# Output projection as seven half products per pair of blocks, with features on partitions

## The reference

```python
qkv = silu(x @ qkv_w.T)                    # 32 heads x (q, k, v) x 128
attn = linear_attention(q, k, v, decay)    # causal, no softmax
xf = attn * rsqrt(mean(attn * attn) + EPS) # over all 4096 features
gate = sigmoid(x @ gate_w.T)
x = layernorm(x + (gate * (norm_w * xf)) @ out_w.T)   # 4096 -> 512
x = layernorm(x + ffn(x))                  # 512 x 512 base, 8 low rank experts, router
```

## Time and profile before

| | us |
|---|---|
| median of three runs | 1011.59 |
| the profiled execution | 1010.33 |
| its span, first to last instruction | 1008.5 |
| TensorE busy | 994.7 |
| VectorE busy | 765.4 |
| ScalarE busy | 662.9 |
| GpSimd busy | 344.3 |

### The profile page before, as it was taken

How to read it: one execution, slowest core, us unless ns; L and a number is a source line. 1 busy time by engine, 2 the same in 40 slices (tenths; PEclk the granted TensorE clock), 3 DMA queues, 4 the chain that set the end, 5 groups by cost and what they waited for, 6 DMA issues and landing times.

```text
span 1008.5 us, 15712 instructions
## 1 busy us (share of the span) xinstructions
PE 994.7 (99%) x5620; PEld 873.8 (87%) x5620; DVE 765.4 (76%) x1102; ACT 662.9 (66%) x1108; POOL 344.3 (34%) x329
## 2 busy tenths in 40 slices
PE   8999999999999999999999999999999999999996
PEld 6878998889888898889988898888988899888886
DVE  6777875787857966778757878578677787699885
ACT  6577754787467764677647874677647786477644
POOL 1453232441443223432323414342224323321462
PEclk9999999999999999999999999999999999999999
DMA  6111121111211111111111102111111121110402
GB/s 209 34 59 57 51 70 43 50 50 30 71 43 50 50 56 49 60 50 58 53 54 58 50 30 71 42 50 51 50 50 63 40 68 51 42 51 22 147 22 84
DMA packets 48813, 57.77 MB, mean 57 GB/s; under 512 B 4320, under 2 KB 40032, under 8 KB 48736
## 3 DMA queue, kind: packets, MB, share of 16 engines
q1 hardware_dynamic: 48736, 56.77, 18.1%
HBM read 54.65 MB, written 2.10 MB: 56 GB/s over the span
## 4 chain that ended last, share of the span: by engine, by line
PE 92%; DVE 2%; ACT 2%; issue 1%; POOL 1%; DMA 1%; SPq 0%; POOLq 0%; ACTq 0%; DVEq 0%
PE ps L1834 20%; PE ps L1835 19%; PE ps L1836 19%; PE ps L1828 10%; PE ps L1829 9%; PE ps L1830 9%; PE ps L1926 2%; PE ps L1941 1%; PE ps L1928 1%; PE ps L1943 1%; DMA acc<-xt 1%; DMA stage<-stream 0%; DVE xl L1030 0%; POOL rstd L1726 0%; ACT wh L388 0%
## 5 line engine op out<-in xcount | busy, mean ns | idle before, releaser
L1834 PE MATMUL ps<-xh,wh 128*128 128x512 f32 x658 | 261.9, 398 | 0.6 <-ACT stg L436 0.6
L1835 PE MATMUL ps<-xl,wh 128*128 128x512 f32 x658 | 257.2, 391 | 0.0
L1836 PE MATMUL ps<-xh,wl 128*128 128x512 f32 x658 | 256.1, 389 | 0.0
L1743 POOL TENSOR_TENSOR stage<-stage 128x512 f32<-128x512 f32 x61 | 85.6, 1403 | 323.6 <-DMA stage<-stream 323.3
L1763 POOL TENSOR_TENSOR sqacc<-sqacc,sq 128x512 f32<-128x512 f32 x64 | 92.4, 1444 | 279.0 <-ACT sq L547 279.0
L1030 DVE TENSOR_TENSOR wl<-stage,wh 128x1024 fp32r<-128x1024 f32 (+2 forms) x145 | 155.7, 1084 | 32.6 <-ACT wh L388 32.5
L388 ACT ACTIVATE wh<-stage 128x1024 fp32r<-128x1024 f32 (+2 forms) x145 | 122.1, 855 | 55.8 <-PE ps L1830 33.7
L1836 PEld LDWEIGHTS ps<-xh,wl 128*128 128x128 f32 x658 | 123.6, 188 | 26.6
L1834 PEld LDWEIGHTS ps<-xh,wh 128*128 128x128 f32 x658 | 123.6, 188 | 24.1 <-issue 1.0
L1835 PEld LDWEIGHTS ps<-xl,wh 128*128 128x128 f32 x658 | 123.9, 188 | 22.0
L1834 PE MATMUL ps<-wh,xh 128*128 128x256 f32 (+1 forms) x416 | 121.0, 291 | 0.0
(11 more groups left out here) (201 smaller groups left out, 2193.7 us busy)
## 6 DMA issues: line engine op xcount, KB each, us to landing
stage<-stream SPq DMA_DIRECT2D x61, 384.0 KB, 3.3
stage<-stream SPq DMA_DIRECT2D x42, 256.0 KB, 2.9
stage<-stream SPq DMA_DIRECT2D x63, 128.0 KB, 2.1
dec<-decay SPq DMA_DIRECT2D x32, 192.0 KB, 2.3
acc<-xt SPq DMA_DIRECT2D x8, 256.0 KB, 6.2
v<-x SPq DMA_DIRECT2D x8, 256.0 KB, 5.6
out<-acc SPq DMA_DIRECT2D x8, 256.0 KB, 2.0
sfull<-lora_router SPq DMA_DIRECT2D x1, 512.0 KB, 4.7
```

The costliest lines, as they stand in the source:

```text
L1743: nc.gpsimd.tensor_tensor(stage[:, s, 1:5:3, :], stage[:, s, 0:6:5, :], stage[:, s, 7:8, :].broadcast_to([P, 2, U]), ALU.add).then_inc(t_p ...
L1834: nc.tensor.matmul(dst, wt[0], mv_[0], start=start, stop=False, skip_group_check=True)
L1835: nc.tensor.matmul(dst, wt[0], mv_[1], start=False, stop=False, skip_group_check=True)
L1836: return nc.tensor.matmul(dst, wt[1], mv_[0], start=False, stop=stop, skip_group_check=True)
```

## The change

The projection of the groups 0 to 6 becomes one product by the same seven-product scheme, transposed: out_w's blocks are stationary, y's token halves move (512 columns), and the result has features on partitions. It is done for two halves j of the 512 output features; the half products (i, j) go to banks 0 to 3 (j = 0) and 4 to 7 (j = 1).

- oa and ob are loaded as blocks with unit sums. ScalarE multiplies them in `stage` by the norm weight before GpSimd's sums (`scale_rows`, eight copies of 256 columns a group).
- The seven operands of y are made of sums by GpSimd (`y_sums`, four operations of 1024 columns) and split 1024 columns at a time (`operand_hi`, `operand_lo`), into yh/yl and, once the scores are done, kh/kl and qh/ql.
- ScalarE copies banks onward (`o_u2_copy`, `o_u3_copy`). Product 5 isn't saved: VectorE adds it out of its bank to two quarters of the sum at once (`out_add` with p5), the others from theirs.
- The ring of weight slots gets a new layout (period of 70 units a group). va and vb, oa and ob are split as A, A, B, B. va's half B moves from QK3 to the next QK0; oa's and ob's halves B are split in the output stage, and `splits_of_load` lets SP reload their places only then; gate weights go there.
- The sum is turned in the tail: `turned(t)`, four transposes for each of 8 token tiles, read by `scaled`. x's tiles `res` take the place of acc there; `last_addition` goes.
- In `scores` the two matmuls of the second key tile come before the last of the first.

Below, "..." stands for what is left out.

```diff
+OUT_STEPS = [(1, 0), (1, 1), (5, 0), (6, 0), (6, 1), (5, 1), (2, 0), (2, 1), (7, 0), (7, 1), (3, 0), (3, 1), (4, 0), (4, 1)]
...
             def v1(g):        # ScalarE
                 n, h = block_no(g, V1), HG * g
                 u2_copy(n)
                 v21_out(n - 1)
+                part(h - 1, 1)
+                square(h - 1, 1)
                 p5_copy(n)
-                if g > 0:
-                    out_rows_hi(g, "oa", 0)
+                sums_hi(g, "oa", "A")
                 u3_copy(n)
-                if g > 0:
-                    out_rows_hi(g, "oa", 1)
                 v11_out(n)
+                sums_hi(g, "ob", "A")
                 v22_out(n)
...
                 scores_hi(h, 0)
+                operand_hi(g, 5)
                 v12_out(n)
                 v21_out(n)
-                values_hi(h)
+                operand_hi(g, 6)
 
             def output(g):    # ScalarE
                 h = HG * g
+                o_u2_copy(g, 0)
+                scores_hi(h, 1)
+                o_u2_copy(g, 1)
+                operand_hi(g, 2)
+                sums_hi(g, "oa", "B")
+                sums_hi(g, "ob", "B")
+                o_u3_copy(g, 0)
+                operand_hi(g, 7)
+                o_u3_copy(g, 1)
+                operand_hi(g, 3)
+                operand_hi(g, 4)
+                values_hi(h)
                 sums_hi(g, "g01", "A")
...
+            def out_add(g, name, j):
...
+                if name == "p5":
+                    dst = acc_t[:, 2 * j + 1, :].rearrange("p (e n) -> p e n", e=2)
+                    nc.vector.tensor_tensor(dst, dst, ps[:, bank, :].unsqueeze(1).broadcast_to([P, 2, W]), ALU.add)\
+                        .then_inc(o_added, 1)
+                    return
...
             def v1(g):        # VectorE
...
+                sums_lo(g, "oa", "A")
                 mask(h, 0)
+                mask_sum(h, 0)
                 c22_add(n)
-                mask_sum(h, 0)
+                sums_lo(g, "ob", "A")
                 c12_add(n)
...
                 scores_lo(h, 0)
+                operand_lo(g, 5)
                 mask(h, 1)
+                mask_sum(h, 1)
+                operand_lo(g, 6)
 
             def output(g):    # VectorE
                 h = HG * g
+                scores_lo(h, 1)
+                operand_lo(g, 2)
+                out_add(g, "p5", 0)
+                sums_lo(g, "oa", "B")
+                sums_lo(g, "ob", "B")
+                operand_lo(g, 7)
+                out_add(g, "c11", 0)
+                out_add(g, "p5", 1)
...
+            def y_sums(g):    # GpSimd
+
+                h = HG * g
+                a11, a12, a21, a22 = y_full[1], y_full[2], y_full[7], y_full[4]
+                pool.wait_ge(y_done, 2 * (h - 1) + 2)
...
+                nc.gpsimd.tensor_tensor(y_temp, a21, a22, ALU.subtract).then_inc(y_sum, 1)
+                nc.gpsimd.tensor_tensor(a21, a21, a11, ALU.subtract).then_inc(y_sum, 1)
+                pool.wait_ge(y_sum, 4 * (g - 1) + 2)
+                pool.wait_ge(y_lo, operand_no(g, 1))
+                nc.gpsimd.tensor_tensor(a11, a11, y_temp, ALU.subtract).then_inc(y_sum, 1)
+                pool.wait_ge(y_sum, 4 * (g - 1) + 3)
+                pool.wait_ge(y_lo, operand_no(g, 5))
+                nc.gpsimd.tensor_tensor(y_temp, a12, a11, ALU.subtract).then_inc(y_sum, 1)
...
+                    sums(g, "oa")
                     add_squares(h - 1, 0)
+                    sums(g, "ob")
                     add_squares(h - 1, 1)
+                    y_sums(g)
                     sums(g, "g01")
...
+            def out_product(g, i, j, bank, start, stop):    # TensorE
+
+                slot = unit_slot(g, ("oa", "ob")[j], UNIT[i])
+                hi, lo = y_operand[i]
+                for k in range(2):
+                    last = mm3_onto(ps[:, bank + S_B * j, :], (wh[:, slot, tile(k)], wl[:, slot, tile(k)]),
+                                    (hi[:, k, :], lo[:, k, :]), start and k == 0, stop and k == 1)
+                last.then_inc(o_done, 1)
+
             def output(g):
...
+                pe.wait_ge(y_lo, operand_no(g, 5))
+                pe.wait_ge(cp5, n + 1)
+                out_product(g, 5, 0, B5, True, True)
+                pe.wait_ge(y_lo, operand_no(g, 6))
+                pe.wait_ge(o_cp01, 2 * (g - 1) + 1)
+                out_product(g, 6, 0, B1, False, False)
...
+                pe.wait_ge(t_lo, part_no(g, "ob", "B"))
+                pe.wait_ge(y_lo, operand_no(g, 2))
+                out_product(g, 2, 0, B0, False, True)
...
+            def turned(t):
...
+                for j in range(4):
+                    last = nc.tensor.transpose(ps[:, TURN_BANK[t], tile(j)], acc_t[:, j, tile(t)], ident[:, :])
+                last.then_inc(acc_turned, 1)
```

More of the change, by code:

```diff
@@ L71, in load_no, with unit_slot, part_no, splits_of_load @@
     return len(LOADS0) + (g - 1) * len(LOADS) + LOADS.index(name)
+def unit_slot(g, name, u):
+    if name in PAIRED:
+        a, b = PAIRED[name]
+        place = a + u if u < 3 else b + u - 3
+    else:
+        place = PLACE[name] + u
+    return (place + PERIOD * g) % RING
+def part_no(g, name, part):
+    m = load_no(g, name)
+    if name in ("va", "oa"):
+        return 2 * m + (1 if part == "A" else 3)
+    if name in ("vb", "ob"):
+        return 2 * m + (0 if part == "A" else 2)
+    return 2 * m + (1 if part == "A" else 2)
+def splits_of_load(m):
+    if len(LOADS0) <= m < TAIL_LOAD and LOADS[(m - len(LOADS0)) % len(LOADS)] in ("va", "oa"):
+        return 2 * m + 3
+    return 2 * m + 2
+def out_no(g, i, j):
+    return len(OUT_STEPS) * (g - 1) + OUT_STEPS.index((i, j)) + 1
+def added_no(g, name, j):
+    return len(OUT_ADDS) * (g - 1) + OUT_ADDS.index((name, j)) + 1
+def operand_no(g, i):
+    return 7 * (g - 1) + OUT_ORDER.index(i) + 1
 def block_no(g, place):
@@ new lines, in scale_rows @@
+            def scale_rows(g, name):
+                m = load_no(g, name)
+                s = m % 2
+                act.wait_ge(t_in[s], 32 * ((m + 1) // 2))
+                if g == 1 and name == "oa":
+                    act.wait_ge(const_in, 16 * (CONSTS - 1))
+                for units, head in ((slice(0, 8, 7), HG * (g - 1)), (slice(3, 6, 2), HG * (g - 1) + 2)):
+                    for k in range(2):
+                        row = stage[:, s, units, tile(k)]
+                        last = copy(row, row, scale=nw[:, head + k:head + k + 1])
+                last.then_inc(t_scaled, 1)
@@ L721, in output @@
[L721 to L723 removed]
             def g01(g):
                 n = block_no(g, G01)
[L727 removed]
+                if g > 0:
+                    sums_hi(g, "qk1", "A")
+                    u2_copy(n)
+                    sums_hi(g, "qk1", "B")
+                    p5_copy(n)
+                else:
                     p5_copy(n)
                     sums_hi(g, "qk1", "A")
[L730 removed]
+                u3_copy(n)
@@ L1844, in features, with values @@
                 return last
-            def values(i, bank, step, start, stop):
+            def values(g, i, bank, step, start, stop):
                 for t in range(2):
@@ L1862, in product @@
                 if b in (V0, V1):
-                    last = values(i, bank, b - V0, start, stop)
+                    last = values(group_of(n), i, bank, b - V0, start, stop)
                 else:
-                    last = features(i, bank, NAMES[b], start, stop)
+                    last = features(group_of(n), i, bank, NAMES[b], start, stop)
                 last.then_inc(p_done[i], 1)
@@ L1934, in attention @@
                 pe.wait_ge(s_lo, 2 * h + e + 1)
+                if h > 0 and h % HG == 0:
+                    pe.wait_ge(o_added, added_no(h // HG, "c21" if e else "c12", 1))
                 for b in (2 * e, 2 * e + 1):
```

480 lines of the change are left out of this document (256 added, 224 removed).

## The result

The changed kernel takes 1023.46 us (median of four runs, 1022.20 to 1024.28), the kernel before 1011.43 beside it: ratio 1.0119, 95% interval 1.0104 to 1.0134. It is slower by 12 us; 1015.0 was forecast, and 1021 was the end of the range. The profiled execution took 1024.28 us with a span of 1022.5, against 1010.33 and 1008.5 before.

A forecast was written before the change was run, and what follows sets the result against it. TensorE's gapless instruction stream was taken as the bound. Loop -0.1 (19.1 us gained, given back in waits) and tail +3.4 made +3.3 on the profiled 1010.33: 1013.6, by the median 1014.9, told as 1015.0; range 1004 to 1021.

The forecast's parts named there:

- Part 1: Output stage: 96 matmuls become 84, 2.72 us less per group, -19.1 us over seven groups.
- Part 2: Other engines' added work per group: some 7 us VectorE, 10 ScalarE, 16 GpSimd; a 1024-column GpSimd sum takes 2.39 us.
- The sum of work costs nothing: Whole group: the other engines have enough idle time in 118.2 us for the added work; only order can cost.
- Part 3: GpSimd sums and VectorE splits from two SBUF inputs: whichever begins first holds the other off for its whole length, 2.39 us.
- Rival A: Output stage: no holding, product 2 starts only 1.5 us late; -5.1 us, 1006.5; chance 0.26.
- Part 4: Group 4's output stage: TensorE waits 1.5 us before product 6, 2.8 late by product 2; 2.7 taken per group.
- After that nothing is late: Output stage behind product 2: operand 7 and the additions come in time, no further wait.
- Covered by 1.3 us; beyond that each us costs itself: Gate weights, loaded from 503.6 instead of 488: ready at 514.4, wanted at 515.7.
- Rival D: Gate weights' first half also late or holdings pile up: 1 to 3 us more per group, 1025 and more; chance 0.06.
- Part 5: Tail: eight tiles turned at 0.52 us each, +4.2, less gaps given back: +3.4 us; from 961.31 on all shifts whole.
- Part 6: Scores: the reordered matmuls only move the place of a longer step, 2.6 us at most either way; 0 taken.
- The loop: Seven groups: 2.7 us of waits against 2.72 us saved in each, -0.1 us in all.

The follow-up runs named there:

- e13: Changed kernel with ScalarE's scaling of the output weights cut from 128x256 to 128x1 elements an instruction: 1023.42 us, ratio to the kernel before 1.0125.
- e1: Changed kernel with GpSimd's four operand sums replaced by four-byte memsets, projection computed from other operands: 1013.65 us, ratio to the kernel before 1.0019.
- e8: e6 with GpSimd's first operand sum waiting until VectorE has split oa's first half: 1018.14 us, ratio to the kernel before 1.0065.
- e16: Changed kernel, in QK1 ScalarE squares and VectorE gates before splitting the first half of qk2's weights: 1019.12 us, ratio to the kernel before 1.0077.
- e2: Changed kernel with the fifth product's addition moved behind the second halves of oa and ob on VectorE: 1016.48 us, ratio to the kernel before 1.0050.
- e5: Changed kernel with GpSimd's sum of operand 6 second and that of operand 7 third: 1023.85 us, ratio to the kernel before 1.0115.
- e15: e14 with ScalarE's split of operand 2 ahead of the second bank copy: 1012.65 us, ratio to the kernel before 1.0019.
- e7: e6 with oa's second half split at V1's end instead of in the output stage: 1021.72 us, ratio to the kernel before 1.0104.
- e9: e6 with VectorE's split of the first half of qk1's weights ahead of the last two additions: 1015.75 us, ratio to the kernel before 1.0051.
- e17: e15 with the swap of e16, a complete kernel: 1008.68 us, ratio to the kernel before 0.9970.
- e14: Changed kernel, sums regrouped so three follow the last gated half, fifth product added later, VectorE's operand 7 split ahead of it, last sum behind that split: 1013.76 us.
- e6: Changed kernel with the edits of e5 and e2 together: 1016.10 us, ratio to the kernel before 1.0046.
- e10: e8 and e9 together: 1018.04 us, ratio to the kernel before 1.0073.

## Why the prediction was wrong

The direction and the mechanism in the output stage were right; the profiled difference is 13.95 us where 3.3 was forecast.

- **Part 1**, 2.72 us less per group: agrees with the table, where waits of 2.4 to 2.5, and 0.1 in the step behind each, leave groups 4 to 6 at 0 to +0.07.
- **Part 2**: GpSimd's 1024 columns take 2.41 us (2.39 forecast). The estimate of 2.4 us beside it was a slip: the 2.6 cycles an element of the Trainium skill (GPSIMD Engine Reference, section on elementwise cycle accounting) make an estimate of 2.2 us at the 1.2 GHz that it reckons with, and the measured 2.41 decides. The fifth product's addition steps 1.13 (506.29 to 507.42), as taken. "The sum of work costs nothing" held for the scaling (e13), and that order would decide was right. But I walked 18 us of it and no more.
- **Part 3**, the holds: shown. A 2.41 us sum holds a split for its length (3.19 instead of 0.95). By the Trainium skill (SBUF — State Buffer, who interferes with whom) that is the rule for an instruction with two SBUF inputs; the trace agrees for 2.4 us as for 1.3, and e1 puts the price of the four sums at 9.8 us. Rival A fell with it.
- **Part 4**, the walk: 1.5 before product 6 and 1.3 before product 2 forecast; 1.26 to 1.28, 1.15 to 1.25 and up to 0.3 before product 3 measured in groups 2 to 6, 2.4 to 2.8 us per group. I had VectorE's split of oa's first half go ahead of the first sum; the sum won by 0.04 us, for which the walk had 2.5 instead of 2.8. By e8 that near tie decides little, since a pause for the scores lies behind it. Groups 1 and 7 fell out of the pattern: wl 0.67 and q 1.91 in the one, 1.29 for c22 in V1 in the other, so that they take 1.7 and 2.0 us more than before, the other five together 1.0. I had walked group 4 alone.
- **Part 4, the step that failed**: "After that nothing is late", and "Covered by 1.3 us; beyond that each us costs itself". I followed the late load of the gate weights to the next block and stopped. The gate block is in time, as forecast (the load started at 508.67, its first products don't wait). But the loads share two stage places: g23's starts at 521.87 where it started at 502.94, and qk2's at 527.90, 6.5 us ahead of the first part of the attention in QK1 (534.40) where it had been 9.2 us ahead (520.14 and 529.30). The sums of qk2's weights, 1.0 us of them holds, end 1.5 us behind that part, where they had ended 1.9 us ahead of it. There, in the block behind the gate block, a split stands in front of a square: +6.5 us, 5.7 of it in waits over 0.3. Rival D had a third wait "at the start of the gate block", 0.06: the right kind at the wrong place. The rows, SyncE's issues first, then GpSimd's sums of qk2's weights, of the changed kernel:

```profile
521.87 0.33 SPq L374 DMA_DIRECT2D stage<-stream  x1
...
527.90 0.33 SPq L374 DMA_DIRECT2D stage<-stream  x1
```

```profile
531.98 1.46 POOL L1842 TENSOR_TENSOR stage<-stage 128x512 f32<-128x512 f32 x1 [2.69 <-DMA stage<-stream]
...
535.19 0.74 POOL L1849 TENSOR_TENSOR stage<-stage 128x256 f32<-128x256 f32 x1
```

and of the kernel before:

```profile
502.94 0.33 SPq L306 DMA_DIRECT2D stage<-stream  x1
...
520.14 0.33 SPq L306 DMA_DIRECT2D stage<-stream  x1
```

```profile
526.29 1.08 POOL L1750 TENSOR_TENSOR stage<-stage 128x256 f32<-128x256 f32 x1
```

e16 shows that the split in front of the square makes most of these waits. That it takes a late load as well is seen across the traces. Fourteen of them have the changed kernel's order in QK1 (it, e1, e2, e5 to e15). In their groups 4 and 6 the third set is 1.0 us in all seven cases where qk2's load starts 7.1 us or less ahead of the first part, and none over 0.2 in eighteen of the nineteen where it starts 8.0 or more ahead (0.3 in the other); the two between show 0.2 and 0.3. In groups 2 and 5 up to 0.8 stays before the scores at 8.0 and more, which no run explains. No run moved the load alone by enough to test it (e7, e9).
- **The start**, 0: +0.84 measured. 0.59 of it is the same place in group 0. qk1's second half is split there in two pieces now (47.84 to 50.23 on VectorE, in one piece 47.51 to 48.74 before), qk2's load starts at 50.26 instead of 48.76, ScalarE stands 2.06 us for its sums instead of 1.51, and TensorE 0.36 us for ScalarE's next copy (59.73). No run takes it apart.
- **Part 5**, tail: +3.4 forecast, +1.9 measured. A second set of transposes in a tile adds 0.40 us (a tile takes 3.61, from 964.49 to 968.10, and took 3.21), not the 0.52 of the first set. That makes 3.2; the 0.60 and 0.2 came back as forecast, and the router's transposes stood 0.93 us for VectorE before (at 982.36), 0.30 now: 1.8. That pause was in the trace of before, and I had written that from 961.31 on all shifts whole.
- **Part 6**, 0 taken: fits, though not tried apart. Behind G23, up to the next group's V1, the difference between the two traces stays within 0.02 us in each group, with scores of several heads in it.

The loop was put at -0.1 and came to +12.1: 6.5 by the step that failed, 4.8 more than forecast in the output stages, 3.7 of it in the two groups, 1 and 7, that fell out of the pattern, and 0.8 at the start. The tail came 1.5 under its forecast.

What stays open: 0.25 us at the start, the waits before the scores in groups 2 and 5, what the later splits of g23's weights in G01 (a part of the change that no run takes back) do to the blocks behind, and whether in e17 the 0.6 us before product 3 comes from the late start of the last sum, as its trace suggests (ScalarE stands for that sum).

## What to carry to other kernels

An engine with 20% idle in the mean can have none in the stretch where an edit puts its work: take busy time over the stretch before summing over the group, and when it is full, take work or holds out of that queue (e1), or put first in it what the bottleneck waits for first (e2 and e14, 7 us each). Another order of the producers gave nothing (e5). When a load starts later, follow it through every stage place that it shares, until some load comes that doesn't start later, and at each look for what stands in queue in front of work that was ready. Walk the first and the last group too.

## What the runs showed of the hardware

GpSimd's add of two fp32 operands takes 0.74, 1.29 and 2.41 us for 256, 512 and 1024 columns. While one runs, a VectorE instruction with two SBUF inputs doesn't start, and two that wait take turns: in the changed kernel the held split ran between the sums of 491.02 and 493.39, and the second sum shows 3.13 us. VectorE's additions with one input in PSUM kept their 0.68 us beside GpSimd (495.83). What I had not expected: taking away a hold of 2.2 us (e8 against e6, e10 against e9) gained nothing and by the medians cost 2 us. By e8's trace the hold had covered a pause, and the sums behind it moved onto splits that had none.
